# Cross attention of a perceiver block: scores in row groups, values per head, a new order of evacuations

## The reference

```
q = (layernorm(x) @ Wq + bq), k = (ctx @ Wk + bk), v = (ctx @ Wv + bv)     # 16 heads of 8
scores = q @ k^T / sqrt(8);  masked positions get the lowest float
w = softmax(scores); masked positions of w set to 0
x = x + (w @ v, heads joined) @ Wo + bo
```

## Time and profile before

| | us |
|---|---|
| Median of the runs | 622.74 (622.25 to 626.61) |
| Span of the profiled execution, first to last instruction | 607.4 |
| Cross attention, first scores to last statistics | 15.9 to 196.1 |
| Recurrence and expert layers behind it | 196.1 to 607.4 |

### The profile page before, as it was taken

The page is one execution under the profiler, slowest core; times in us unless marked ns, Lnnn a source line. Parts: engine busy times, 40 slices in busy tenths (PEclk is TensorE's granted clock), DMA queues, the critical chain, the costliest instruction groups (busy, mean ns, idle before and its releaser), DMA issues.

```text
span 607.4 us, 14280 instructions
## 1 busy us (share of the span) xinstructions
PE 536.6 (88%) x4254; PEld 437.6 (72%) x4254; DVE 364.3 (60%) x795; ACT 304.5 (50%) x732; POOL 214.7 (35%) x206
## 2 busy tenths in 40 slices
PE   2899999999996887799997699996899997699994
PEld 2678777877774563599963499973389994389992
DVE  3578787787877676645535745532944552954552
ACT  2567767676774831366621266631066650066550
POOL 3433242432420202541550640541362352363252
PEclk9799999999999987799999799996799999899999
DMA  5100000004930002110111110112010012010015
GB/s 134 29 11 18 9 9 17 9 17 137 332 94 2 0 1 70 32 36 7 41 60 42 26 38 10 36 39 71 5 45 24 23 37 83 1 49 24 18 42 151
DMA packets 30587, 27.73 MB, mean 46 GB/s; under 512 B 4608, under 2 KB 24384, under 8 KB 30528
## 3 DMA queue, kind: packets, MB, share of 16 engines
q1 hardware_dynamic: 26432, 18.59, 10.5%
q0 software_dynamic: 4096, 8.40, 4.8%
HBM read 20.68 MB, written 6.29 MB: 44 GB/s over the span
## 4 chain that ended last, share of the span: by engine, by line
PE 59%; DVE 18%; DMA 7%; issue 6%; ACT 6%; SPq 1%; POOL 1%; DVEq 0%; POOLq 0%; ACTq 0%
PE bank L748 19%; PE bank L761 18%; PE bank L564 5%; PE bank L592 3%; DVE nmax L858 3%; DMA cur<-token_rows 3%; ACT pp L420 2%; PE bank L573 2%; DVE rden L877 2%; DVE ohr L1047 2%; PE bank L543 2%; DMA token_rows<-ysort,token_i 2%; DMA qm<-token_rows,token_i 2%; PE bank L560 1%; PE bank L546 1%
## 5 line engine op out<-in xcount | busy, mean ns | idle before, releaser
L1096 DVE SCALAR_TENSOR_TENSOR hh<-th,bank 128x512 f32<-128x512 f32 x124 | 85.2, 687 | 118.8 <-ACT th L514 118.8
L761 PE MATMUL bank<-w,hh 128*128 x992 | 135.6, 280 | 3.0 <-DVE hh L1096 3.0
L748 PE MATMUL bank<-qm,w_piece 128*128 x992 | 134.8, 280 | 0.0
L761 PEld LDWEIGHTS bank<-w,hh 128*128 128x128 f32 x992 | 121.7, 193 | 4.6 <-issue 4.1
L748 PEld LDWEIGHTS bank<-qm,w_piece 128*128 128x128 f32 x992 | 122.5, 194 | 1.8 <-issue 1.3
L514 ACT ACTIVATE th<-bank 128x512 f32<-128x512 f32 x124 | 74.1, 597 | 84.8 <-PE bank L748 84.8
L505 ACT COPY w_piece<-w 128x512 f32 x124 | 75.8, 611 | 60.7 <-DVE piece_tile L1069 60.0
L323 POOL TENSOR_TENSOR qm<-qT,head_of 128x1024 f32<-128x1024 f32 x32 | 60.2, 1904 | 110.6 <-ACT qT L408 110.6
L361 POOL DMA_INDIRECT token_rows<-ysort,token_i x64 | 62.2, 971 | 101.1 <-DVE ysort L1106 94.8
L420 ACT ACTIVATE pp<-bank,nmax 128x128 f32<-128x128 f32 x256 | 73.5, 375 | 17.8 <-DVE nmax L858 17.8
L644 PE MATMUL bank<-trib,onesb 128*128 128x512 bf16 x308 | 82.2, 428 | 0.0
(11 more groups left out here) (186 smaller groups left out, 551.3 us busy)
## 6 DMA issues: line engine op xcount, KB each, us to landing
w<-in_L_ffn_W_dram SPq DMA_DIRECT2D x1, 4096.0 KB, 14.6
cur<-token_rows SPq DMA_DIRECT2D x16, 256.0 KB, 3.9
cx<-in_ctx_dram SPq DMA_DIRECT2D x16, 128.0 KB, 2.1
token_rows<-cur SPq DMA_DIRECT2D x1, 1024.0 KB, 5.1
qm<-token_rows,token_i POOLq DMA_INDIRECT x64
token_rows<-ysort,token_i POOLq DMA_INDIRECT x64, 2.2
out_dram<-xs SPq DMA_DIRECT2D x4, 256.0 KB, 2.8
xs<-in_x_dram SPq DMA_DIRECT2D x1, 768.0 KB, 5.7
```

The source lines that it names most:

```text
L748: last = mm(banks[2 + j % 2][:, c * P:(c + 1) * P], w1_piece[:, j % 2, c * P:(c + 1) * P], xT[:, ds(tile_of[j] * P, P)], start=True, stop= ...
L761: last = mm(banks[6 + j % 2][:, 0:D], hh[:, j % 2, c * P:(c + 1) * P], w2[:, ds(e * FF + c * P, P)], start=(c == 0), stop=(c == FC - 1))
L1096: v.scalar_tensor_tensor(hh[:, j % 2, :], th[:, j % 2, :], 1.0, banks[2 + j % 2][:, :], ALU.add, ALU.mult).then_inc(s["h_ready"], 1)
```

## The change

The scores of one tile now go into four banks (0 to 3) at once. Bank r holds heads 4r to 4r+3, and its products use rows 32r to 32r+31 of the array alone: `qm` holds for each j the tokens of q with only the rows of heads j, 4+j, 8+j, 12+j (`own_head`), 256 columns per sequence. The products of the four banks alternate in program order. The mask products use 64 rows each, the two halves by turns (`mask_i` is loaded twice, one DMA more; `pair_rows` holds the identity twice). All of scores(t) wait for all exponentials of t-1. `nmax` and `pp` have four buffers.

For the values, `vm` holds for each head a 32-column block in which only its own 8 columns are not zero (a stride of 40 within 160 columns places them), and four products j = 0 to 3 add up in one group of 32 partitions; the denominators are made in the same way from `head_ones`. That makes 64 products of 64 columns per tile where there were 16 of 256. `own_heads`, `diag` and `od` go; `attention_out` reads bank 6, `residual` multiplies by `keep_any` as it adds.

Banks: 4 for the inputs' transposes and for probabilities 0 and 3, 5 for v and probabilities 1 and 2, 6 for values and out projection, 7 for q and k. Copies of the turned probabilities: 0, 1, 2 on DVE, 3 on ACT. POOL now also normalises (`xln_tile`, tile t+3) and adds the out bias. q and k are projected two tiles ahead, v one. `xin` and `xT` of the expert layers become buffers of their own, where they lay in `qm`. The old functions are printed above; of the diff, the added lines:

```diff
+vm = sb("vm", [P, 2, BT * 4, 160])
+nmax = sb("nmax", [P, 4, 4])
+pp = sb("pp", [P, 4, 512])
...
-    with eng.Fori(2, NT - 3, 2) as t:
+    with eng.Fori(2, NT - 5, 2) as t:
         body(t, 0, first=False, last=False)
         body(t + 1, 1, first=False, last=False)
-    body(NT - 2, 0, first=False, last=False)
-    body(NT - 1, 1, first=False, last=True)
+    for t in range(NT - 4, NT):
+        body(t, t % 2, first=False, last=t == NT - 1)
...
+    g.memset(vm[:], 0.0)
...
+    def queries(t, u):
+        pool.wait_ge(s["qk_evac"], t + 1)
         if not isinstance(t, int) or t >= 2:
+            for r in range(4):
+                pool.wait_ge(scored[r], t - 1)
         for b in range(BT):
+            last = g.tensor_tensor(
+                qm[:, u, b, :, :], qT[:, u, b * S:(b + 1) * S].unsqueeze(1).broadcast_to([P, 4, S]),
+                own_head[:].unsqueeze(2).broadcast_to([P, 4, S]), ALU.mult)
+        last.then_inc(s["qm_ready"], 1)
...
+    def xln_tile(t, u):
+        if not isinstance(t, int) or t >= 2:
+            pool.wait_ge(s["tr_done"], t - 1)
+        g.tensor_scalar(xln[:, u, :], tile_of(t), mean[:, ds(t, 1)], rstd[:, ds(t, 1)],
+                        ALU.subtract, ALU.mult).then_inc(s["xln_ready"], 1)
+    def add_out_bias(t):
+        pool.wait_ge(s["xln_ready"], t + 1)
+        g.tensor_tensor(tile_of(t), tile_of(t), bor[:], ALU.add).then_inc(s["xo_ready"], 1)
+    def pool_tile(t, u, first, last):
+        if not (isinstance(t, int) and t + 2 >= NT):
+            queries(t + 2, u)
+        if not (isinstance(t, int) and t + 3 >= NT):
+            if first:
+                pool.wait_ge(s["rstd_ready"], 2)
+            xln_tile(t + 3, 1 - u)
+            add_out_bias(t + 3)
+    pool.wait_ge(s["rstd_ready"], 1)
+    xln_tile(0, 0)
+    xln_tile(1, 1)
+    xln_tile(2, 0)
...
     def evac_qk(t, u):
+        act.wait_ge(s["qk_done"], t + 1)
         if not isinstance(t, int) or t >= 2:
...
     def tile(t, u, first, last):
+        if not (isinstance(t, int) and t + 1 >= NT) and not first:
+            evac_qk(t + 1, 1 - u)
+        if not (isinstance(t, int) and t + 2 >= NT) and not first:
+            evac_inputs(t + 2, u)
         if not first:
+            evac_pt3(t - 1)
+        for r in range(4):
+            exp_scores(t, r, first)
...
+    def scores(t, u, first):
+        pe.wait_ge(s["qm_ready"], t + 1)
+        pe.wait_ge(s["qk_evac"], t + 1)
+        if not first:
+            pe.wait_ge(s["exp_done"], 4 * t)
+        for r in range(4):
+            half = slice((r % 2) * S, (r % 2 + 1) * S)
+            mm(banks[r][:, :].rearrange("p (k t) -> p k t", k=4), pair_rows[half, :],
+               mask_bias[half, :].unsqueeze(1).broadcast_to([S, 4, T]), start=True, stop=False)
         for k in range(4):
+            b, pair = k // 2, k % 2
+            for r in range(4):
+                rows_of = slice(32 * r, 32 * r + 32)
+                last = mm(banks[r][:, k * T:(k + 1) * T],
+                          qm[rows_of, u, b, 2 * pair:2 * pair + 2, :].rearrange("p j s -> p (j s)"),
+                          kT[rows_of, u, b * T:(b + 1) * T], start=False, stop=(k == 3))
+                if k == 3:
+                    last.then_inc(scored[r], 1)
+    def transpose_probs(t, r):
+        pe.wait_ge(s["exp_done"], 4 * t + r + 1)
+        if r == 3:
+            pe.wait_ge(s["a_evac"], NT if isinstance(t, int) and t + 3 >= NT else t + 4)
+        elif r == 0 and (not isinstance(t, int) or t >= 1):
+            pe.wait_ge(s["pt_evac_act"], t)
+        elif r == 1:
+            pe.wait_ge(s["v_evac"], NT if isinstance(t, int) and t + 1 >= NT else t + 2)
+        elif r == 2:
+            pe.wait_ge(s["pt_evac_dve"], 3 * t + 2)
...
+    def values(t, u):
+        pe.wait_ge(s["pt_evac_dve"], 3 * t + 3)
+        pe.wait_ge(s["pt_evac_act"], t + 1)
+        pe.wait_ge(s["v_evac"], t + 1)
+        if not isinstance(t, int) or t >= 1:
+            pe.wait_ge(s["x_updated"], t)
         for which in range(2):
+            for b in range(BT):
+                for j in range(4):
+                    at = (2 * b + j // 2) * P + (j % 2) * S
+                    for r in range(4):
+                        lhsT = vm[:, u, b * 4 + r, 32 * j:32 * j + 32] if which == 0 else head_ones[:, j, :]
+                        c = which * P + b * S
+                        last = mm(banks[6][32 * r:32 * r + 32, c:c + S], lhsT, ppT[:, r, at:at + S],
+                                  start=(which == 0 and b == 0 and j == 0),
+                                  stop=(which == 1 and b == 1 and j == 3))
         last.then_inc(s["od_done"], 1)
...
     def tile(t, u, first, last):
+        scores(t, u, first)
         if not first:
+            transpose_probs(t - 1, 3)
         if not last:
+            project_v(t + 1, 1 - u)
+        if not (isinstance(t, int) and t + 2 >= NT):
+            project_qk(t + 2, u)
         if not first:
+            values(t - 1, 1 - u)
+        transpose_probs(t, 0)
         if not first:
             project_out(t - 1, 1 - u)
+        transpose_probs(t, 1)
+        if not (isinstance(t, int) and t + 3 >= NT):
+            transposes_in(t + 3, 1 - u)
+        transpose_probs(t, 2)
...
+    def values_evac(t, u):
+        dve.wait_ge(s["v_done"], t + 1)
         if not isinstance(t, int) or t >= 2:
+            dve.wait_ge(s["od_done"], t - 1)
+        v.tensor_tensor(vm[:, u, :, :].rearrange("p n (j x) -> p n j x", x=40)[:, :, :, 0:HD],
+                        banks[5][:, 0:BT * D].rearrange("p (n j d) -> p n j d", j=4, d=HD),
+                        bvr2[:].rearrange("p (n j d) -> p n j d", j=4, d=HD), ALU.add) \
+            .then_inc(s["v_evac"], 1)
...
     def tile(t, u, first, last):
+        if not first:
+            evac_pt(t - 1, 2)
         scores_max(t, 0, first)
         scores_max(t, 1, first)
+        if not last:
+            values_evac(t + 1, 1 - u)
         scores_max(t, 2, first)
+        scores_max(t, 3, first)
         if not first:
             attention_out(t - 1, 1 - u)
+        evac_pt(t, 0)
         if not first:
             residual(t - 1, 1 - u)
+        evac_pt(t, 1)
...
```

More of the change, by code:

```diff
@@ L312, in _ @@
             g.memset(nf16[:, :, 0:1], 0.0)
[L313 to L317, removed]
+            for c in range(2):
+                g.tensor_tensor(pair_rows[:, c * S:(c + 1) * S], ident[:, 0:S], ident[:, S:P], ALU.add)
+            for j in range(4):
+                last = g.memset(head_ones[:, j, j * HD:(j + 1) * HD], 1.0)
@@ L331, in _ @@
+            pool.wait_ge(s["rstd_ready"], 1)
+            xln_tile(0, 0)
+            xln_tile(1, 1)
+            xln_tile(2, 0)
+            pool.wait_ge(s["w_loaded"], W_ATT)
+            for t in range(3):
+                add_out_bias(t)
+            pool.wait_ge(s["consts_dve"], 1)
+            queries(0, 0)
+            queries(1, 1)
+            for t in range(NT):
+                pool_tile(t, t % 2, t == 0, t == NT - 1)
             wait_normalised(pool, 0, 2)
@@ L408, in evac_qk @@
[L408 to L415, removed]
+                    act.wait_ge(s["qm_ready"], t - 1)
+                    for r in range(4):
+                        act.wait_ge(scored[r], t - 1)
@@ L416, in exp_scores @@
+                a.activation(qT[:, u, :], banks[7][:, 0:P], ACT.Identity, bias=bqc[:, 0:1],
+                             scale=float(HD) ** -0.5)
+                a.activation(kT[:, u, :], banks[7][:, P:3 * P], ACT.Identity, bias=bkc[:, 0:1],
+                             scale=1.0).then_inc(s["qk_evac"], 1)
+            def exp_scores(t, r, first):
+                n = 4 * t + r
                 act.wait_ge(s["nmax_ready"], n + 1)
-                if not (first and i < 2):
-                    act.wait_ge(s["pt_done"], n - 1)
+                if not first:
+                    act.wait_ge(s["pt_done"], n - 3)
@@ L454, in _ @@
[L454 removed]
+            evac_pt3(NT - 1)
             def evac_tiles():
@@ L549, in scores @@
-            def scores(t, u, i, first):
-                n = 4 * t + i
-                b, half = i // 2, i % 2
-                if half == 0:
-                    pe.wait_ge(s["qm_ready"], 2 * t + (b + 1))
-                if i == 0:
-                    pe.wait_ge(s["k_evac"], t + 1)
-                if not (first and i < 2):
-                    pe.wait_ge(s["exp_done"], n - 1)
-                bank = banks[i % 2]
-                mm(bank[:, :].rearrange("p (k t) -> p k t", k=4), pair_rows[:],
-                   mask_bias[:].unsqueeze(1).broadcast_to([P, 4, T]), start=True, stop=False)
-                for k in range(4):
-                    c = ((b * HEADS) + (half * 4 + k) * 2) * S
-                    last = mm(bank[:, k * T:(k + 1) * T], qm[:, u, c:c + P], kT[:, u, b * T:(b + 1) * T],
-                              start=False, stop=(k == 3))
-                last.then_inc(s["s_done"], 1)
@@ new lines, in scores_max, with evac_pt @@
+            def scores_max(t, r, first):
```

(18 more changed lines are left out.)

252 lines of the change are left out of this document (78 added, 174 removed).

## The result

The changed kernel takes 682.27 us (median of four runs, 681.43 to 687.88), the kernel before 623.12 us on the same chip (622.25 to 626.61): ratio 1.0981, 95% interval 1.0916 to 1.1047. I had forecast 639 with a range up to 670: the direction was right, the size was not. Some executions take over 1.5% longer than the fastest of their kernel, at a lower granted clock, and the ratios leave them out.

A forecast was written before the change was run, and what follows sets the result against it. TensorE (busy 88%) was taken to bound the kernel before; a cycle of waits at 12.2 us a tile moved the stage's end from 196.1 to 212.4 us, so 622.7 + 16.3 = 639 us, range 614 to 670.

The forecast's parts named there:

- (f): ACT's exponentials of banks 2 and 3, then evac_qk(t+2): 2.8 us a tile.
- (a): TensorE's mask and score products with overlapping row groups: 1.58 us a tile.
- (c): ACT's copy of the transposed bank 3 of tile t-1: 0.59 + 0.07 us.
- (d): TensorE's values(t-1), 64 products in column groups: 2.2 us, 2.64 with tail, tiling changes and handoff.
- (e): DVE's values_evac(t+1), waiting for the values, ahead of the maxima of banks 2 and 3: 1.11 us.
- (g): POOL's queries(t+2), standing ahead of xln_tile(t+3), then that xln: 1.75 us a tile.
- (h): TensorE's transposes_in(t+3), waiting for xln, and transposes of bank 2, ahead of the next scores: 0.82 us.
- rival E: TensorE's granted clock falls to its lower level in its idle gaps; doubled steps add 4 us a tile, 700 us; 6%.
- rival B: TensorE's values are bound by instruction issue, 3.8 us instead of 2.2: +26, 665 us; 20%.
- rival C: Row groups don't overlap in TensorE's masks (0.9 us) and scores (3.5 us): +42, 681 us; 9%.
- Second path: Scores through values, values_evac, maxima, attention_out, out projection, residual, bank 1 copy, transposes: 10.9 us, deciding for tiles 13 and 14.
- Rival D: POOL isn't the gate, values stream at 1.8 us: about 10.5 us a tile, 617 us, or 612 with more; 15%.

The follow-up runs named there:

- B: Changed kernel plus eight filler bf16 products of 512 columns at each of TensorE's two waiting places per tile: 638.98 us, ratio 1.0503 to the kernel before.
- D: Changed kernel with the 16 score products in bank order, one row group after another instead of alternating: 751.04 us, ratio 1.2336 to the kernel before.
- I in turn: Kernel of I with score products of one row group after another instead of alternating: 624.91 us, ratio 1.0087 to the kernel before.
- C: Changed kernel with the third context loaded before the later weights instead of behind their 22 DMAs: 664.35 us, ratio 1.0909 to the kernel before.
- G: Changed kernel with the loads of w1 and w2 moved behind the attention stage: 685.32 us, ratio 1.1026 to the kernel before.
- A: Changed kernel with POOL's xln_tile(t+3) and bias ahead of queries(t+2): 646.74 us, ratio about 1.05 to the kernel before, no interval.
- F: Changed kernel with DVE's values_evac moved behind the maxima of banks 2 and 3: 659.83 us, ratio 1.0609 to the kernel before.
- H: Changed kernel with the edits of A and F together: 621.96 us, ratio 1.0032 to the kernel before.
- I: Changed kernel with A, C, F, G, project_out at the end of PE's tile, attention_out and residual behind DVE's copies: 599.11 us, ratio 0.9649 to before.
- E: Changed kernel again without any edit, measured beside later runs: 684.12 us, ratio 1.1038 to the kernel before.

## Why the prediction missed

The path was right and its durations were those of another clock. From the trace after (110.04 to 124.22) and from B (97.11 to 109.67), step by step, with the handoff from ACT to POOL counted in (f):

| step | forecast | after | B, clock 1.00 |
|---|---|---|---|
| (a) masks and scores | 1.58 | 2.48 | 1.64 |
| (b) transposes of bank 3 | 0.67 | 0.69 | 0.69 |
| (c) copy, to the start of values | 0.66 | 1.00 | 1.00 |
| (d) values, to values_evac | 2.64 | 2.13 | 2.13 |
| (e) values_evac, maxima | 1.11 | 1.13 | 1.13 |
| (f) exponentials, evac_qk | 2.96 | 2.88 | 2.88 |
| (g) POOL, to transposes_in | 1.59 | 2.19 | 2.18 |
| (h) transposes, to the next masks | 0.82 | 1.68 | 0.91 |
| sum | 12.03 | 14.18 | 12.56 |

- **The step that failed** is the sentence "with durations at full clock". I had it as rival E, at 6%, with doubled PE steps and 4 us a tile. In this tile the lower level cost 0.84 us in (a) and 0.77 in (h): 1.6; the next tile, of 15.52 us, had slow projections and transposes of bank 3 too. On average it is 14.80 - 12.60 = 2.2 a tile, 31 us in 14 tiles: two thirds of the 46 us by which the stage ended later than forecast. The rows I held against it were no evidence, since the kernel before had no such gaps; the earlier trace rows showed the effect, and I gave it a low chance although my own cycle put two gaps of 2 us into every tile. The granted clock was 0.74 with two waits of 1.7 and 2.4 us a tile, and 1.00 with fillers in them. The Trainium skill, "TensorE: Matmul & The Clock Gate", section "A second HAM failure mode: psum-queue depth-cycling", describes a kernel that idles briefly between groups of products and swings between the two levels; the trace after with its 0.74 and its two waits a tile agrees. E's own size was too high: doubling (a), (b), (d) and (h) as I summed them would be 5.7 us, not 4, and only some of PE's steps ran at the lower level, for 2.2.
- **(c)** missed PE's own list: after the transposes of bank 3 come v and then q and k, 1.2 us, and these end after ACT's copy (values start at 114.21, the copy ended at 113.80). +0.34.
- **(g)** queries 1.17 (taken 1.1), xln 0.80, not 0.38: I priced a POOL operation by its elements. By L323's 1.86 ns an element, the three would be 1.19 us; I took 1.48 and called it "by L323". A single operation of 128x128 with two scalar columns is dearer than one of 128x256 (0.61). +0.6.
- **(d)** rival B is out, and so, for this case, is the floor of 25 ns that the Trainium skill gives (named at (d) of the forecast): 128 records of 64 columns in column groups take 1.92 us (114.21 to 116.13), 15 ns for a load and its product; my lower bound of 1.8 was the near one. -0.5.
- **(a)** at full clock (B) within 0.06; rival C is out (D, and I in turn). **(b), (e), (f)** right within 0.1.
- **Start**: scores(1) at 35.47 against 28.4. I had priced SP's queue by one DMA more, but not what moved behind it: transposes_in(2) now precede the first scores, and the third context stands behind the later weights (C, where the marks come at 17.48 and 29.07, against 17.2 and 28.4). +7.1.
- **Second path and tail**: the tail was 15.86 against 15.8. Tiles 13 and 14, without an xln ahead, took 13.5 and 12.9 us, 1.3 to 1.9 less than the mean, as forecast (1.3), but from the higher level. Tile 13 is next to the stall (G).
- **Rival D** (faster) needed the gate of POOL away: it is the order of A that takes it away, not a quicker POOL, and it was not enough (12.55 us a tile). Only with F as well (H, 10.29) does a tile come below the break-even of 10.85.
- **The sum**: forecast end of stage 212.4, measured 258.7, of which 7.1 come from the start, 39.2 from the tiles and 0.1 from the tail. The trace before lay 15.3 us under the median, and I called that launch and end; 2 us are launch and end, and 10 lie in the part behind the stage, which differs from chip to chip as said above; the remaining 3 are not traced. As 16.3 was added to the median this cost the forecast little.

What stays open: how long the stall at the loop's end lasts (3.3 and 5.2 us in two traces of the same kernel), what besides PE's waits lowers the clock (D, I in turn), and the 0.5 us a tile that H keeps above the theory's upper figure.

## What to carry to other kernels

When a change takes work from the bounding engine and adds links between engines, write the new cycle down and look for TensorE's waits in it; if they are long, recompute with TensorE's steps at the lower clock, since the earlier trace rows no longer holds. Then move what is not needed yet behind what is waited for, on every queue: here two swaps of two lines in POOL's and DVE's lists were worth 0.10 of the time, as much as the change had cost. Read the granted clock of the stage again after each edit. Filler products are a good test of what the clock costs, but belong only where a wait is.

## What the runs showed of the hardware

- Four row groups of 32 rows with f32 products of 128 columns: 32 records in 1.10 us alternated (I), 2.74 in turn (I in turn), both at clock 1.00: 2.5 times, not four times.
- Four column groups: 128 pairs of load and product of 64 columns in 1.92 us (114.21 to 116.13 after), 15 ns a pair, half of the nearest row for full-width ones. The Trainium skill, "TensorE: Matmul & The Clock Gate", section "Wait — 56ns, not 53.3ns?", gives a floor of about 25 ns between starts; with column groups these rows lie below it, and the measurement decides.
- TensorE waited 1.7 to 2.4 us twice a tile in the trace after, and its granted clock was 0.74, a mix of 1.2 and 2.4 GHz; with products in these waits (B) it was 1.00, and in I, where the longest wait from 30 to 150 us was 1.3, too. But in I in turn it fell to 0.75 and 0.86 in two tiles around which the longest wait was 0.5.
- At the end of the hardware loop PE stood still for 1.4 to 5.2 us, and went on 2.6 to 2.8 us after a packet of 16 KB had started on the instruction queue (after, E, A, G, H).
- POOL: in the trace after, 128x128 f32 with mean and rstd as columns took 0.80 us, a product of 128x256 f32 0.61, a sum of 128x128 0.45.
